# Routed experts at the end of a two-layer attention and FFN block: where expert numbers are loaded, what feeds the router, which engine splits the weights, and fill-in matmuls

## Chip, cores and metric

One core of one Trainium2 chip. The metric is the device time in microseconds (us) of one execution. The core has five instruction queues that run side by side and meet only at semaphores: TensorE (PE, with its weight loads PEld), VectorE (DVE), ScalarE (ACT), GpSimd (POOL) and SyncE (SP, which only starts transfers). A queue is worked off in order: what waits holds up all that stands behind it.

## What is computed

The stream x has 1024 tokens of 256 values. Two layers each add a gated cross attention and a gated FFN of normalised x. The change touches the end: the second layer's FFN, and the second attention only where weight work is laid beside it.

```python
x = x + tanh(g_xattn[1]) * L1_xattn(layernorm(x), ctx)
x = x + tanh(g_ffn[1]) * L1_ffn(layernorm(x))
# L1_ffn: 16 routed experts, top 2, and one shared expert
logits = xt @ Wr.T + bias;  probs = softmax(logits)
topk_val, topk_idx = top_k(probs, 2);  w = topk_val / (sum(topk_val) + EPS)
y[t, e] = (silu(xt @ Wg[e]) * (xt @ Wu[e])) @ Wd[e]
routed = sum over the chosen two of w * y
shared = (silu(xt @ sWg) * (xt @ sWu)) @ sWd
```

## The kernel before, in words

**Two-part numbers.** Each matmul operand is kept as an upper part (a rounded copy, `hi`) and a lower part (the rest, `lo`), and a product is three matmuls: hi*hi, hi*lo, lo*hi. ACT makes upper parts by copying (L1065 is its copy helper), DVE or POOL makes lower parts by subtracting.

**Second attention (`attention1`).** A loop over eight head pairs. POOL's only work in it is `normalise`: two multiplications for a pair (L430). After it `context_and_output` forms 16 context blocks, then eight output tiles of 128 tokens, each added to the stream `X` by DVE (`add_output`).

**Expert weights.** 16 experts and one shared expert are loaded in five groups (`WGROUPS`), the first at the start of `attention1`. Before the change all of them are split after the context: ACT copies the shared expert and experts 0 to 12 in one run, POOL subtracts the shared one and the even experts (L495), DVE the odd ones, one between two output tiles (`output_and_weights`, L1887). Experts 13 to 15 follow later.

**Layer norm 3.** For tiles 0 to 3, then 4 to 7, DVE computes statistics and an inverse root in a chain of small dependent operations (L1411 to L1418). Tiles are normalised by DVE (two) and ACT (two), transposed by PE (L578), copied by ACT to `xs[0]`, and DVE subtracts for `xs[1]` (`lower_part`).

**Routing.** The router needs whole numbers: POOL adds `xs[0]` and `xs[1]` to `xnT1` (`whole_stream`, L438), 512 tokens at a time, and PE multiplies by `wr` (`router`, L924). Then there is one chain: DVE picks two experts (`choice`, L1735 to L1750, its end is the count CHOSEN), PE ranks tokens within experts (`ranks`), DVE counts blocks, PE adds starts (`positions`), DVE gets each token's slot, a block number and a one-hot (`pk`, `beq`, `onehot`, L1764 to L1777), POOL forms `btok` from `beq` (L524), PE turns these into a list of tokens for each slot (`slot_tokens`), DVE converts it (`idxf`, `idx`, `eid`, L1785 to L1791). The slots are grouped into 31 blocks of 128, each of one expert. Work of the shared expert (`shared_gate_up`, `shared_hidden`, `shared_down`) stands between these steps on all engines.

**Blocks.** POOL gathers the 128 rows of a block by an indirect transfer (L532) into one of six buffers. PE takes blocks in 16 pairs: pairs 0 to 14 of two, the last of one. In pair i it loads two expert numbers from `eid` to registers (`expert_of`, a value_load), then `block_gate_up` of block 0 (six matmuls, L987 to L989, which find their weights by the register), `hidden_transposes(i-1)` (L998), `block_gate_up` of block 1, `block_transposes(i+2)` (L968), `block_down(i-1)` (six matmuls, L1011 to L1013). `block_down(i-1)` waits for `hTb_lo`, which comes from the hidden transposes by an ACT copy and a DVE subtraction (L1439). The results go to DRAM pair by pair.

**End.** After the last pair POOL gathers two result rows for each token (16 indirect transfers, L540), DVE adds them, SP writes the output.

`bridge(count, bank)` is a helper that was there before: PE multiplies a 128x128 identity by itself `count` times into an unused bank (L565). One such multiplication appears as two records in the trace.

Of the kernel before, what the change touches and what calls it, by code (L numbers as in the profile page):

```python
# [7 lines left out]
P = 128  # L8
# [46 lines left out]
def build(nc, x, kvT, kvTrot, kv, cosT, sinT, cosR, sinR, cosQ, sinQ, attn0, attn1, ffn0, ffn1,  # L55
          router0, router1, bias1, gates, ident_d, iota_d, tables, out):
    with ExitStack() as ctx:
# [183 lines left out]
        class SparseSems:  # L241
            def __init__(s):
# [3 lines left out]
                s.whi, s.wlo_p, s.wlo_d = sem(p + "whi"), sem(p + "wlo_p"), sem(p + "wlo_d")  # L246
# [16 lines left out]

        def width(i):
            return min(2, NBLK - 2 * i)
# [11 lines left out]
        def _(sp):  # L277
# [87 lines left out]
            for i in range(NPAIR):  # L365
                nb = width(i)
                sp.wait_ge(sparse.by, i + 1)
                sp.dma_start(y_dram[2 * i * P:(2 * i + nb) * P].rearrange("(b p) d -> p b d", p=P),
                             yout[:, i % YB, 0:nb * DM].rearrange("p (b d) -> p b d", b=nb)).then_inc(
                    sparse.y_out[i % YB], 16)  # L370
# [9 lines left out]
        def _(pool):  # L380
# [43 lines left out]
            def normalise(s):  # L424

                with pool.Fori(0, HP - 1) as i:
                    for h in range(2):
# [4 lines left out]
                            ALU.mult).then_inc(s.p, 1)  # L432

# [56 lines left out]
            def sparse_ffn():  # L490
                s = sparse

                def lower_weights(dst, raw, upper, count):
                    pool.wait_ge(s.whi, count)
                    nc.gpsimd.tensor_tensor(dst, raw, upper.bitcast(F32), ALU.subtract).then_inc(s.wlo_p, 1)  # L495

# [24 lines left out]
                for k in range(2):  # L521
                    for part in range(2):
                        tok = table[:, TTOK + part * NT:TTOK + (part + 1) * NT].unsqueeze(2).to_broadcast([P, NT, NCOL])
                        nc.gpsimd.tensor_tensor(btok[:, k * NT:(k + 1) * NT, part, :], beq[:, k * NT:(k + 1) * NT, :], tok,  # L524
                                                ALU.mult).then_inc(s.btok, 1)
# [3 lines left out]
                for j in range(NBLK):  # L529
                    if j >= XG:  # L530
                        pool.wait_ge(s.bt, (j - XG) // 2 + 1)
# [22 lines left out]
        def _(pe):  # L554
# [345 lines left out]
            def sparse_ffn():  # L900
                s, l = sparse, ln[3]

                def shared_gate_up(h):
                    tk = slice(h * HALF, (h + 1) * HALF)
                    for m in range(2):
                        for c in range(NCH):
                            col = (2 * c + m) * INTER
                            last = product(psum[2 * h + m][:, :], cut(WS, slice(None), slice(col, col + INTER)),
# [11 lines left out]
                def router(g):  # L920
                    pe.wait_ge(l.whole, l.before_whole + g + 1)
                    for t in range(4 * g, 4 * g + 4):
                        for c in range(NCH):
# [26 lines left out]
                def slot_tokens():  # L950
                    pe.wait_ge(s.btok, 4)
# [8 lines left out]
                def block_transposes(i):  # L960
                    for b in range(width(i)):
                        j = 2 * i + b
                        pe.wait_ge(s.got[j % XG], 16 * (j // XG + 1))
                    if i >= 2:
                        pe.wait_ge(s.bx, i - 1)
                    for b in range(width(i)):
                        for c in range(NCH):
                            last = nc.tensor.transpose(psum[2 + i % 2][:, b * DM + c * P:b * DM + (c + 1) * P],  # L968
                                                       xg[:, (2 * i + b) % XG, c * P:(c + 1) * P], ident[:])
                    last.then_inc(s.bt, 1)  # L970

                def expert_of(j):
# [55 lines left out]
                shared_down(2)  # L1028
                shared_down(3)
                slot_tokens()  # L1030
                pe.wait_ge(s.wlo_p, 11)
                pe.wait_ge(s.wlo_d, 6)
                pe.wait_ge(s.routed_dve, EXPERTS_OF)
# [29 lines left out]
        def _(act):  # L1063
# [43 lines left out]
            def context(s):  # L1107
                for b in range(NB):
                    act.wait_ge(s.c, b + 1)
                    copy(PT[0][:, :, b * S:(b + 1) * S],  # L1110
                         psum[b % 8][:].rearrange("p (h s) -> p h s", h=HP)).then_inc(s.c_hi, 1)

# [74 lines left out]
            def attention1():  # L1187
# [19 lines left out]

                body(0, first=True)
                with act.Fori(1, HP - 1) as i:
# [5 lines left out]
                context(s)  # L1215
# [68 lines left out]
            def sparse_ffn():  # L1284
                s = sparse

                def expert_upper(e):
                    copy(WE[:, e, 0, :], WE_raw[:, e, 1, :]).then_inc(s.whi, 1)

                def shared_gates(h):  # L1290
                    act.wait_ge(s.gu, 2 * h + 1)
                    nc.scalar.activation(silu1[:, h, :], psum[2 * h][:], ACT.Tanh, scale=0.5).then_inc(s.tanh, 1)
# [35 lines left out]
                act.wait_ge(s.ws, 16)  # L1328
                copy(WS[0][:], WS_raw[:]).then_inc(s.whi, 1)
                for k in range(4):  # L1330
# [3 lines left out]
                normalise(3, 0)  # L1334
                transposed_tiles(3, 0, (0, 1))
# [661 lines left out]
```

## Time and profile before

| | |
|---|---|
| median of 3 runs | 552.73 us (551.34 to 553.9) |
| the profiled execution | 552.05 us |
| its span in the trace | 550.3 us |
| busy: PE, DVE, ACT, POOL | 465.8, 400.2, 194.3, 172.8 us |
| mean granted clock of TensorE | 0.937 |

All times of rows count from the start of the span. In a timeline a row is: start, duration, engine, line, operation, out<-in with shapes, how many records were merged (x4), and in square brackets how long the engine had been idle before it and what ended that. The granted clock is 1.00 at 2.4 GHz and 0.50 at 1.2 GHz. 1.75 us of the profiled execution lie outside its span.

### The profile page before, as it was taken

To read this page: it belongs to the slowest core of one execution; us is meant where nothing else is said; L and a number is where in the kernel's file an instruction comes from. 1 tells how busy PE (TensorE), PEld (TensorE's weight loads), DVE (VectorE), ACT (ScalarE), POOL (GpSimd) and SP (SyncE) were. 2 spreads that over 40 slices of the span, in tenths; PEclk is the share of its full clock that TensorE was granted. 3 is DMA by queue.
4 is the path that set the end of the run, shared out by engine and by line. 5 is a ranking of instruction groups with operands and counts; after the bars stand their busy time and mean duration, and the time that the engine had idled before them with its cause. 6 is when DMAs were issued, how large, how long until landed. Compare 5 with 4: busy or idle time off the path is not lost.

```text
span 550.3 us, 8996 instructions
## 1 busy us (share of the span) xinstructions
PE 465.8 (85%) x3126; PEld 384.8 (70%) x3126; DVE 400.2 (73%) x838; ACT 194.3 (35%) x370; POOL 172.8 (31%) x149
## 2 busy tenths in 40 slices
PE   4499999999999999989998999999986818777600
PEld 4368667766865899978897888877986617776500
DVE  6988889889988946798679476879896774444323
ACT  3134222132332702434322456546914104445300
POOL 3815101101122001636530112120744476442064
PEclk9899999999999999999999999998997767999955
DMA  8302201220321100001105242223105014443234
GB/s 270 105 1 76 77 16 61 76 76 0 133 74 62 71 1 1 1 29 59 29 1 193 75 147 85 89 88 114 58 2 183 1 47 107 134 128 94 77 104 134
DMA packets 20287, 42.42 MB, mean 77 GB/s; under 512 B 3393, under 2 KB 10817, under 8 KB 20257
## 3 DMA queue, kind: packets, MB, share of 16 engines
q1 hardware_dynamic: 18000, 35.85, 19.6%
q0 software_dynamic: 2256, 6.16, 4.7%
q8 instruction: 19, 0.31, 0.2%
q14 instruction: 12, 0.09, 0.0%
HBM read 35.85 MB, written 6.16 MB: 76 GB/s over the span
## 4 chain that ended last, share of the span: by engine, by line
PE 52%; DVE 19%; issue 17%; POOL 6%; DMA 3%; ACT 2%; POOLq 0%; SPq 0%; DVEq 0%; ACTq 0%
PE ps L557 9%; PE ps L558 9%; PE ps L559 9%; PE ps L709 8%; POOL fg L540 2%; POOL probs L430 2%; PE ps L605 2%; PE ps L657 2%; PE ps L987 2%; DVE xT_lo L1439 2%; PE ps L989 1%; PE ps L988 1%; PE ps L615 1%; DMA W<-attn 1%; DVE rstd L1417 1%
## 5 line engine op out<-in xcount | busy, mean ns | idle before, releaser
L430 POOL TENSOR_TENSOR probs<-probs,rowrec 128x512 f32<-128x512 f32 x28 | 28.7, 1045 | 169.1 <-DVE rowrec L1477 168.9
L1065 ACT ACTIVATE PT_hi<-ps 128x512 fp32r<-128x512 f32 (+1 forms) x64 | 35.3, 604 | 54.6 <-PE ps L615 52.4
L557 PE MATMUL ps<-xs_hi,A_hi 128*128 128x512 f32 x128 | 52.4, 409 | 1.5 <-DVE xs_lo L1430 1.5
L558 PE MATMUL ps<-xs_lo,A_hi 128*128 128x512 f32 x128 | 50.4, 393 | 0.0
L559 PE MATMUL ps<-xs_hi,A_lo 128*128 128x512 f32 x128 | 50.3, 393 | 0.0
L1439 DVE TENSOR_TENSOR PT_lo<-ps,PT_hi 128x512 fp32r<-128x512 f32 (+1 forms) x64 | 40.8, 684 | 5.3 <-ACT PT_hi L1065 5.1
L532 POOL DMA_INDIRECT xg<-xn_rows,idx x31 | 29.6, 953 | 26.3 <-PE ps L968 18.6
L557 PE MATMUL ps<-N_hi,PT_hi 128*128 128x256 f32 x128 | 36.3, 284 | 0.0
L558 PE MATMUL ps<-N_lo,PT_hi 128*128 128x256 f32 x128 | 36.2, 282 | 0.0
L559 PE MATMUL ps<-N_hi,PT_lo 128*128 128x256 f32 x128 | 35.9, 281 | 0.0
L1465 DVE TENSOR_REDUCE rowmax<-ps 128x8 f32<-128x512 f32 x32 | 21.8, 683 | 16.8 <-PE ps L605 16.8
L987 PE MATMUL ps<-experts_split,xT_hi 128*128 x62 | 21.2, 341 | 13.6 <-DVE xT_lo L1439 13.2
L1065 ACT ACTIVATE G<-ps 128x512 f32<-128x512 f32 x32 | 18.9, 594 | 38.6 <-PE ps L709 34.8
L605 PEld LDWEIGHTS ps<-kbd,G 128*64 128x64 f32 x512 | 28.2, 137 | 5.6 <-issue 4.7
L605 PE MATMUL ps<-kbd,G 128*64 128x128 f32 x512 | 31.4, 275 | 0.0
L557 PEld LDWEIGHTS ps<-xs_hi,A_hi 128*128 128x128 f32 x128 | 24.3, 190 | 7.7 <-DVE xs_lo L1430 1.9
L1439 DVE TENSOR_TENSOR hTb_lo<-ps,hTb_hi 128x256 fp32r<-128x256 f32 (+1 forms) x16 | 6.7, 416 | 30.2 <-ACT hTb_hi L1065 30.2
L1085 ACT ACTIVATE probs<-probs 128x512 f32<-128x512 f32 x32 | 20.1, 629 | 23.6 <-DVE probs L1467 23.5
L559 PEld LDWEIGHTS ps<-xs_hi,A_lo 128*128 128x128 f32 x128 | 24.3, 190 | 5.4
L457 POOL TENSOR_TENSOR PT_lo<-qc,PT_hi 128x512 fp32r<-128x512 f32 x15 | 19.4, 1292 | 26.5 <-ACT PT_hi L1065 26.5
L558 PEld LDWEIGHTS ps<-xs_lo,A_hi 128*128 128x128 f32 x128 | 24.4, 190 | 4.5
L1071 ACT ACTIVATE qb<-X,shift,rstd 128x256 f32<-128x256 f32 x16 | 8.7, 594 | 52.7 <-DVE shift L1418 52.7
(222 smaller groups left out, 1351.4 us busy)
## 6 DMA issues: line engine op xcount, KB each, us to landing
W<-attn SPq DMA_DIRECT2D x8, 704.0 KB, 4.2
W<-attn SPq DMA_DIRECT2D x8, 672.0 KB, 4.0
W<-attn SPq DMA_DIRECT2D x16, 320.0 KB, 4.4
y_rows<-yout SPq DMA_DIRECT2D x15, 256.0 KB, 2.3
WF<-ffn SPq DMA_DIRECT2D x8, 384.0 KB, 4.1
experts_raw<-ffn SPq DMA_DIRECT2D x2, 1536.0 KB, 6.9
experts_raw<-ffn SPq DMA_DIRECT2D x2, 1152.0 KB, 5.8
X<-x SPq DMA_DIRECT2D x4, 256.0 KB, 5.0
```

What stands on the lines that cost most here:

```text
L430: nc.gpsimd.tensor_tensor(part, part, rowrec[:, 4 * h:4 * h + 4, :].unsqueeze(3).to_broadcast([P, 4, 2, L]), ALU.mult).then_inc(s.p, 1)
L532: nc.gpsimd.indirect_dma_start(out=xg[:, j % XG, :], out_offset=None, in_=xn_dram, in_offset=bass.IndirectOffsetOnAxis(ap=idx[:, j:j + 1], ...
L557: nc.tensor.matmul(dst, lhs[0], rhs[0], start=start, stop=False)
L558: nc.tensor.matmul(dst, lhs[0], rhs[1], start=False, stop=False)
L559: return nc.tensor.matmul(dst, lhs[1], rhs[0], start=False, stop=stop)
L605: last = nc.tensor.matmul(psum[6 + h][b * S:(b + 1) * S, t * P:(t + 1) * P], G[:, tok:tok + S], kbd[:, 2 * (4 * h + t) + b, :], start=True ...
L709: last = nc.tensor.matmul(psum[4 + h][a * DC:(a + 1) * DC, :], Wp[:, k, a * DC:(a + 1) * DC], rows[:, a, h * HALF:(h + 1) * HALF], start=( ...
L987: nc.tensor.matmul(out_, hi, w_hi, start=(c == 0), stop=False)
L1065: return nc.scalar.activation(dst, src, ACT.Copy)
L1085: nc.scalar.activation(part, part, ACT.Exp).then_inc(s.exp, 1)
L1439: V.tensor_tensor(dst, src, upper.bitcast(F32), ALU.subtract).then_inc(done, 1)
L1465: V.tensor_reduce(mx, sc, AX, ALU.max).then_inc(s.max, 1)
```

## The change

1. **Expert numbers.** The numbers of pairs 0 and 1 are loaded before `shared_down(2)`; those of pair i+2 inside pair i, one after each `block_gate_up`.
2. **Odd block first.** Pair 0 is now the one with a single block; pair i holds blocks 2i-1 and 2i.
3. **Router.** ACT copies the transposes from PSUM to `xnT1` (`whole`, 256 tokens at a time). POOL's two additions are gone; `router(1)` follows `router(0)` at once. The lower parts `xs[1]` of tiles 4 to 7 are made by POOL, not DVE.
4. **Weight splitting.** ACT splits the shared expert and experts 0 to 3 in the loop of `attention1`, 4 to 6 between context blocks, 7 to 15 after. POOL subtracts all 17.
5. **Order in the routing.** `shared_hidden(1)` moves on DVE from before the block counts to after `onehot`; the weights of the two choices (`mx[4]`, `cw`) move to after `eid`. ACT makes half of `btok`. POOL's `hidden_lower(1)` moves between the third and the fourth gather. On PE `positions` and `slot_tokens` move ahead of shared matmuls.
6. **Fill-ins.** `bridge` of 10, 8, 24 and 10 in `sparse_ffn`.

```diff
+        ODD = NBLK % 2
+        def first_of(i):
+            return max(0, 2 * i - ODD)
         def width(i):
-            return min(2, NBLK - 2 * i)
+            return 1 if ODD and i == 0 else 2
+        SHARED_BANK = (2, 0)
...
@@ POOL, normalise of attention1 @@
+                first = WGROUPS[0][1]
+                pair(0)
+                lower_weights(WS[1][:], WS_raw[:], WS[0][:], 1)
+                with pool.Fori(0, first) as e:
+                    pair(e + 1)
...
+                    lower_weights(lo, raw, hi, e + 2)
+                with pool.Fori(first + 1, HP - 1) as i:
+                    pair(i)
...
@@ POOL, sparse_ffn @@
-                lower_weights(WS[1][:], WS_raw[:], WS[0][:], 1)
-                for e in range(0, 13, 2):
+                for e in range(WGROUPS[0][1], WGROUPS[3][1]):
                     expert_lower(e)
-                pool.wait_ge(at[1].o, NT)
-                whole_stream(3, 0, xnT1)
-                whole_stream(3, 1, xnT1)
-                expert_lower(13)
-                expert_lower(14)
                 hidden_lower(0)
-                expert_lower(15)
-                hidden_lower(1)
+                for b in range(2):
+                    pool.wait_ge(ln[3].hi, ln[3].before + 2 + b + 1)
+                    tk = slice((4 + 2 * b) * P, (6 + 2 * b) * P)
+                    nc.gpsimd.tensor_tensor(xs[1][:, :, tk], xnT1[:, :, tk], xs[0][:, :, tk].bitcast(F32),
+                                            ALU.subtract).then_inc(ln[3].lo, 1)
+                for e in range(*WGROUPS[4]):
+                    expert_lower(e)
...
                 for j in range(NBLK):
+                    if j == 3:
+                        hidden_lower(1)
...
@@ PE, sparse_ffn @@
-                pe.wait_ge(s.wlo_p, 1)
+                pe.wait_ge(s.wlo, 1)
                 pe.wait_ge(l.lo, l.before + 2)
                 shared_gate_up(0)
+                bridge(10, 5)
                 transpose_tiles(3, 1, (6, 7))
                 router(0)
+                router(1).then_inc(s.routed_pe, 1)
+                bridge(8, 5)
                 pe.wait_ge(l.lo, l.before + 4)
-                router(1).then_inc(s.routed_pe, 1)
                 shared_gate_up(1)
                 ranks()
                 shared_down(0)
+                positions()
                 shared_down(1)
-                positions()
+                bridge(24, 2)
+                slot_tokens()
+                bridge(10, 2)
+                pe.wait_ge(s.routed_dve, EXPERTS_OF)
+                of = {i: [expert_of(i, b) for b in range(width(i))] for i in range(2)}
                 shared_down(2)
                 shared_down(3)
-                slot_tokens()
...
                 block_transposes(0)
                 block_transposes(1)
-                of = {}
                 for i in range(NPAIR):
-                    of[i] = [expert_of(2 * i + b) for b in range(width(i))]
...
-                    block_gate_up(i, 0, of[i][0])
-                    if i:
-                        hidden_transposes(i - 1)
-                    if width(i) > 1:
-                        block_gate_up(i, 1, of[i][1])
+                    for b in range(width(i)):
+                        block_gate_up(i, b, of[i][b])
+                        if i + 2 < NPAIR:
+                            of.setdefault(i + 2, []).append(expert_of(i + 2, b))
+                            if width(i) == 1:
+                                of[i + 2].append(expert_of(i + 2, 1))
+                        if i and b == 0:
+                            hidden_transposes(i - 1)
                     if i + 2 < NPAIR:
                         block_transposes(i + 2)
...
@@ ACT, attention1 @@
+                act.wait_ge(sparse.ws, 16)
+                copy(WS[0][:], WS_raw[:]).then_inc(sparse.whi, 1)
+                act.wait_ge(sparse.w[0], 16)
+                with act.Fori(0, first) as e:
+                    body(e + 1)
...
+                    copy(hi, raw).then_inc(sparse.whi, 1)
...
+                context(s, second_group)
...
@@ ACT, sparse_ffn @@
+                def whole(t, bank):
+                    src = psum[bank][:].rearrange("p (c k) -> p c k", c=NCH)
+                    copy(xnT1[:, :, t * P:(t + 2) * P], src).then_inc(s.whole, 1)
+                act.wait_ge(at[1].o, NT)
+                for b in range(2):
+                    act.wait_ge(ln[3].lo, ln[3].before + b + 1)
+                    whole(2 * b, b)
                 shared_gates(0)
                 normalise(3, 1)
+                for b in range(2):
+                    act.wait_ge(ln[3].tp, ln[3].before + 2 + b + 1)
+                    whole(4 + 2 * b, 6 + b)
                 transposed_tiles(3, 1, (6, 7))
                 act.wait_ge(s.w[4], 16)
                 expert_upper(13)
...
+                hidden_upper(0)
                 expert_upper(14)
-                hidden_upper(0)
                 expert_upper(15)
                 shared_gates(1)
...
+                act.wait_ge(s.routed_dve, BLOCK)
+                nc.scalar.activation(btok[:, :, 1, :], beq[:], ACT.Identity,
+                                     scale=table[:, TTOK + NT:TTOK + NT + 1]).then_inc(s.btok_act, 1)
...
@@ DVE, sparse_ffn @@
-                lower_part(3, 1, (6, 7))
+                shared_hidden(0)
                 dve.wait_ge(s.table, 16)
-                shared_hidden(0)
...
-                shared_hidden(1)
                 dve.wait_ge(s.routed_pe, RANKS)
...
+                shared_hidden(1)
                 dve.wait_ge(s.routed_pe, INDEX)
...
-            layer_norm(3, output_and_weights, (0, 1), lower_at=NT - 1)
+            layer_norm(3, lambda t: add_output(at[1], 1, t), (0, 1), lower_at=NT - 1)
```

## Rows read from the trace of the kernel before

**Rows 1.** The page: the chain that ended last, its shares by engine
```profile
PE 52%; DVE 19%; issue 17%; POOL 6%; DMA 3%; ACT 2%; POOLq 0%; SPq 0%; DVEq 0%; ACTq 0%
```
**Rows 2.** Stretches: bounds, us, busy PE, PEld, DVE, ACT, POOL, clock, DMA share, GB/s
```profile
446.00:455.00 9.00, 2.17 (x8) 1.43 (x8) 5.46 (x14) 1.06 (x2) 6.64 (x7) 0.50 0.33 84
455.00:517.00 62.00, 48.71 (x346) 44.29 (x346) 27.50 (x59) 27.23 (x58) 22.92 (x25) 0.96 0.41 110
```
**Rows 3.** Timeline of PE: pair 1, pair 6 and the start of 7, pairs 14 and 15
```profile
457.93 1.05 PE L968 MATMUL ps<-ident,xg 128*128 128x128 f32 x4
458.63 0.56 PE L987 MATMUL ps<-experts_split,xT_hi 128*128 x1
...
480.23 0.39 PE L987 MATMUL ps<-experts_split,xT_hi 128*128 x1 [0.95 <-DVE xT_lo L1439]
...
482.46 0.38 PE L1011 MATMUL ps<-experts_split,hTb_hi 128*128 x1
...
484.42 0.38 PE L987 MATMUL ps<-experts_split,xT_hi 128*128 x1 [0.98 <-DVE xT_lo L1439]
...
515.88 0.38 PE L1011 MATMUL ps<-experts_split,hTb_hi 128*128 x1 [0.31 <-DVE hTb_lo L1439]
...
517.19 0.38 PE L987 MATMUL ps<-experts_split,xT_hi 128*128 x1 [0.34 <-DVE hd L1812]
```
**Rows 4.** Timeline of PE: fill-ins before layer 2, transposes of layer norm 3, router
```profile
303.77 1.73 PE L565 MATMUL ps<-ident 128*128 128x128 f32 x14
...
408.10 1.24 PE L578 MATMUL ps<-ident,qb 128*128 128x128 f32 x8 [1.02 <-DVE qb L1422]
...
419.16 1.94 PE L578 MATMUL ps<-ident,qb 128*128 128x128 f32 x8 [2.18 <-DVE qb L1422]
...
425.04 3.57 PE L924 MATMUL ps<-wr,xnT 128*128 128x16 f32 x16 [0.72 <-POOL xnT L438]
```
**Rows 5.** Timeline of DVE: layer norm 3 and routing
```profile
415.00 1.40 DVE L1411 TENSOR_SCALAR varep<-meanvar 128x4 f32<-128x4 f32 x1
...
428.65 0.29 DVE L1745 TENSOR_TENSOR la<-ps,bias_s 128x128 f32<-128x128 f32 x1 [4.88 <-PE ps L924]
...
429.85 1.80 DVE L1737 SCALAR_TENSOR_TENSOR lb<-lb,table 128x128 f32<-128x128 f32 x1
...
434.27 0.29 DVE L1750 TENSOR_TENSOR mbf<-mk 128x128 bf16<-128x128 f32 x1
...
439.63 0.69 DVE L1772 TENSOR_TENSOR beq<-table,blk 128x512 f32<-128x512 f32 x1
...
445.80 0.23 DVE L1785 TENSOR_REDUCE idxf<-ps 128x32 f32<-128x64 f32 x1 [0.90 <-PE ps L955]
```
**Rows 6.** Timeline of POOL: one pair of attention1, then layer norm 3 and routing
```profile
348.59 2.04 POOL L430 TENSOR_TENSOR probs<-probs,rowrec 128x512 f32<-128x512 f32 x2 [6.50 <-DVE rowrec L1477]
...
413.98 2.40 POOL L438 TENSOR_TENSOR xnT<-xs_hi,xs_lo 128x1024 f32<-128x1024 f32 x1 [8.26 <-DVE xs_lo L1430]
...
428.39 1.27 POOL L503 TENSOR_TENSOR hT_lo<-hid,hT_hi 128x512 fp32r<-128x512 f32 x1
...
429.62 1.88 POOL L495 TENSOR_TENSOR experts_split<-experts_raw,experts_split 128x768 fp32r<-128x768 f32 x1
...
440.47 4.21 POOL L524 TENSOR_TENSOR btok<-beq,table 128x256 bf16<-128x256 f32 x4 [2.30 <-DVE beq L1772]
...
446.53 1.12 POOL L532 DMA_INDIRECT xg<-xn_rows,idx  x1 [1.86 <-DVE idx L1787]
```
**Rows 7.** Timeline of ACT: one pair of attention1; the weights after the context
```profile
346.36 0.38 ACT L1065 ACTIVATE Wp<-ps 96x256 f32<-96x256 f32 x1 [2.12 <-PE ps L586]
...
388.18 9.64 ACT L1065 ACTIVATE experts_split<-experts_raw 128x768 fp32r<-128x768 f32 x13
```
**Rows 8.** Chain in order of time: start, us, what: gather and last result
```profile
447.96 3.96 DMA xg<-xn_rows,idx
...
523.13 1.70 DMA y_rows<-yout
```

More of the change, by code:

```diff
@@ L424, in normalise, with pair @@
             def normalise(s):
-                with pool.Fori(0, HP - 1) as i:
+                def pair(i):
                     for h in range(2):
@@ L432, in normalise, with lower_weights @@
                             ALU.mult).then_inc(s.p, 1)
+                if s is at[0]:
+                    with pool.Fori(0, HP - 1) as i:
+                        pair(i)
+                    return
+                first = WGROUPS[0][1]
[3 more added lines that the diff above has]
+                    pair(e + 1)
+                    lo, raw, hi = (w[:, bass.ds(e, 1), part, :].rearrange("p a c -> p (a c)")
+                                   for w, part in ((WE, 1), (WE_raw, 1), (WE, 0)))
+                    lower_weights(lo, raw, hi, e + 2)
+                with pool.Fori(first + 1, HP - 1) as i:
+                    pair(i)
+            def lower_weights(dst, raw, upper, count):
+                pool.wait_ge(sparse.whi, count)
+                nc.gpsimd.tensor_tensor(dst, raw, upper.bitcast(F32), ALU.subtract).then_inc(sparse.wlo, 1)
             def whole_stream(n, h, dst):
@@ L521, in sparse_ffn @@
                 for k in range(2):
[L522 to L525, printed above, removed]
+                    tok = table[:, TTOK:TTOK + NT].unsqueeze(2).to_broadcast([P, NT, NCOL])
+                    nc.gpsimd.tensor_tensor(btok[:, k * NT:(k + 1) * NT, 0, :], beq[:, k * NT:(k + 1) * NT, :], tok,
+                                            ALU.mult).then_inc(s.btok, 1)
                 pool.wait_ge(s.routed_dve, TOKENS)
@@ L920, in router @@
                 def router(g):
-                    pe.wait_ge(l.whole, l.before_whole + g + 1)
                     for t in range(4 * g, 4 * g + 4):
+                        if t % 2 == 0:
+                            pe.wait_ge(s.whole, t // 2 + 1)
                         for c in range(NCH):
@@ L950, in slot_tokens @@
                 def slot_tokens():
-                    pe.wait_ge(s.btok, 4)
+                    pe.wait_ge(s.btok, 2)
+                    pe.wait_ge(s.btok_act, 1)
                     for q in range(2 * NT):
@@ L1105, in score_weights, with context @@
                      psum[bank][0:rows, 0:sets * P].rearrange("p (c d) -> p c d", c=sets)).then_inc(s.wp_ev, 1)
-            def context(s):
+            def context(s, meanwhile=None):
                 for b in range(NB):
@@ L1206, in body @@
                         t1_and_m(i + 1, 1)
+                first = WGROUPS[0][1]
                 body(0, first=True)
-                with act.Fori(1, HP - 1) as i:
+                act.wait_ge(sparse.ws, 16)
[3 more added lines that the diff above has]
+                    body(e + 1)
+                    hi, raw = (w[:, bass.ds(e, 1), part, :].rearrange("p a c -> p (a c)")
+                               for w, part in ((WE, 0), (WE_raw, 1)))
+                    copy(hi, raw).then_inc(sparse.whi, 1)
+                with act.Fori(first + 1, HP - 1) as i:
                     body(i)
@@ L1214, in attention1, with second_group, expert_upper @@
                 transposed(s, HP - 1, (6, 7))
-                context(s)
+                def second_group(b):
+                    k, after = divmod(b, 4)
+                    if after == 3 and k < 3:
+                        if k == 0:
+                            act.wait_ge(sparse.w[1], 16)
+                        expert_upper(WGROUPS[1][0] + k)
+                context(s, second_group)
+            def expert_upper(e):
+                copy(WE[:, e, 0, :], WE_raw[:, e, 1, :]).then_inc(sparse.whi, 1)
             def experts(n):
@@ L1285, in sparse_ffn @@
                 s = sparse
-                def expert_upper(e):
-                    copy(WE[:, e, 0, :], WE_raw[:, e, 1, :]).then_inc(s.whi, 1)
                 def shared_gates(h):
                     act.wait_ge(s.gu, 2 * h + 1)
-                    nc.scalar.activation(silu1[:, h, :], psum[2 * h][:], ACT.Tanh, scale=0.5).then_inc(s.tanh, 1)
+                    nc.scalar.activation(silu1[:, h, :], psum[SHARED_BANK[h]][:], ACT.Tanh, scale=0.5).then_inc(s.tanh, 1)
                 def hidden_upper(h):
@@ L1326, in block_rows @@
                     copy(yout[:, i % YB, 0:n], psum[6 + i % 2][:, 0:n]).then_inc(s.by, 1)
-                act.wait_ge(s.ws, 16)
-                copy(WS[0][:], WS_raw[:]).then_inc(s.whi, 1)
-                for k in range(4):
+                for k in (2, 3):
                     act.wait_ge(s.w[k], 16)
```

55 lines of the change are left out of this document (24 added, 31 removed).

## Prediction

> **What bounds the kernel now.** I read first the chain that ended last, by engine [rows 1]: TensorE holds half of it, but "issue", time in which an engine waits for nothing that the profile shows, holds 17%. So the next question is where TensorE stands still with its inputs ready. The stretches show two places [rows 2]: before the first pair (446 to 455) TensorE is busy for 2.17 of 9 us and the granted clock is 0.50; in the pairs (455 to 517) it is busy for 48.7 of 62 us at 0.96, and no other engine for more than 27.5. The timelines then show what it waits for. In the pairs, each starts about 4.18 us after the last (58.56 us for 14, from pair 1 to pair 15 [rows 3]). In the routing one chain runs through DVE, PE and POOL until the first gather at 446.53 [rows 6]. What comes before 400 is TensorE's or the attention loop's and has no part in the change but a little work laid into gaps; what comes after the last result (the final gathers) is not touched. So the sum has four terms: time of the first gather, from there to pair 1, the pairs, and the end.
>
> **Cover in the attention.** ACT gets 5 copies in the loop, POOL 5 subtractions. A copy is 9.64 / 13 = 0.74 us [rows 7] and stands where ACT is idle for 2.12 us in each pair [rows 7]. A subtraction is 1.88 us [rows 6] and POOL is idle for 6.50 us in each pair [rows 6]. I cost both at nothing; without that cover it would be 4 x 0.74 = 3 us for ACT. The three copies between context blocks delay the last of them by a few tenths, while TensorE still has output tiles to do: nothing.
>
> **Term 1, the first gather (446.53).**
> (a) Layer norm. The transposes of tiles 0 to 3 stood idle for 1.02 us at 408.10 [rows 4] for DVE, whose turn was lengthened by its expert subtractions; with these gone the wait goes. For tiles 4 to 7 the first small operation of the chain began at 415.00 and took 1.40 us [rows 5], ending with POOL's addition (413.98 + 2.40 = 416.38 [rows 6]). Now it can be held only by POOL's work on expert 12, whose upper part ACT makes after the transposes (now 407.0 to 408.0): I put POOL's end at 413.5. The transposes at 419.16 [rows 4] then start near 416.4, 2.8 earlier.
> (b) Logits. They were read at 428.65 [rows 5], after POOL's sum. Now: transposes 1.24 us as at 408.10 if the fill-ins keep the clock, 1.94 if not [rows 4], then 32 router records, at half clock 3.57 / 16 = 0.22 us each [rows 4], at full clock about 0.12, as the fill-in record has (1.73 / 14 [rows 4]). Logits at 421.5 to 424.8.
> (c) The choice, up to `mbf` (ended 434.56 [rows 5]). One of its operations took 1.80 us, from 429.85 to 431.65, because POOL's weight subtraction ran from 429.62 to 431.50 [rows 5, 6]; the like at 434.27 took 0.29. So an operation of DVE with two SBUF inputs waits for POOL's to end. Now POOL has six there: three of 512 columns (1.27 each) and three of 768 (1.88) [rows 6], 9.4 us from about 421.4 on, when ACT has made the upper part of `hid`. Eight of DVE's operations have two such inputs, and each lets one of POOL's pass first. CHOSEN comes near 432.7, 1.9 earlier than before; without that wait it would be 427. The Trainium skill (SBUF - State Buffer, section "SBUF: two separate sides") has the same as an exclusive lock, held for a whole instruction, and by it moving work to POOL is a cost in itself. By it the sum stays as it stands here.
> (d) From `mbf` to `beq` was 5.07 us [rows 5]; `shared_hidden(1)` (two operations like `beq`, 0.69 each) leaves. I take 3.6: `beq` at 436.3.
> (e) From `beq` to `idxf` was 6.17 us [rows 5], of which POOL's four `btok` took 4.21 [rows 6]. Two are left; the four one-hots, which take turns with them, end 3.5 us after `beq`; `shared_hidden(1)`, 1.4 us, now stands on DVE before `idxf`. That is 441.9, if TensorE is there. But 24 fill-ins stand in its queue before `slot_tokens`: 48 records are 5.9 us at 0.12 and 10.7 at 0.22. Begun near 435.5, they end at 441.3 to 446, and `idxf` comes 1.1 us later. I take a clock that rises on the way: 443.6. The gather follows `idxf` by 0.73: 444.3, **-2.2**. Bounds: -8 (no waits for POOL, full clock), 0 (half clock all along).
>
> **Term 2, gather to pair 1.** It was 458.63 - 446.53 = 12.1 us [rows 3, 6]. Pair 0 needs one block only, but `hidden_lower(1)` (1.27) stands before the fourth gather, and with it `shared_down(2)` and `(3)`, which TensorE must do before the first transposes. The fifth gather is issued after some 5.6 us of four issues of 1.12 and one 1.27, and lands 4.0 later [rows 6, 8], near 10; its transposes follow at half clock or full. 11.2 to 12.5; **-0.4**. The three loads of numbers there fall into TensorE's wait.
>
> **Term 3, the pairs.** From the first matmul of `block_down` to the first of the next pair: 482.46 to 484.42, 1.96 us, with two loads between; 515.88 to 517.19, 1.31, with one [rows 3]. So a load costs 0.65, and six matmuls with their addresses 0.66. In pair 1 at half clock the four transposes (457.93) run into the next matmul (458.63) although two loads lie between [rows 3]: a load hides where TensorE's sequencer is ahead of queued matmuls. At full clock six matmuls take what the sequencer needs to issue them, so it is hardly ever ahead. After the change each load follows six matmuls. What goes is the wait for `hTb_lo` that now stands beside the loads, not under them: the sequencer needs 3 x 0.66 + 2 x 0.65 = 3.28, and what six transposes and their waits need, which lies between 0 and 480.23 to 482.46 less two sixes, 0.91 [rows 3]. A pair takes 3.28 to 4.19; I take the middle, 3.73. Thirteen of them, one without loads or transposes (2.9) and 0.7 for a start at half clock are 52.1 instead of 58.56: **-6.5**.
>
> **Term 4, the end.** The last pair has two blocks now, not one. From 517.19 to the landing of its result (523.13 + 1.70 = 524.83 [rows 8]) were 7.64 us. Six more matmuls (0.7), twice the width for the small operations and a result twice as long add 1.2 to 1.8; **+1.2**, as the clock may hold.
>
> Sum: -2.2 - 0.4 - 6.5 + 1.2 = -7.9 on the profiled execution, 552.05 to 544.15, or 544.0. The median shown is 0.7 above that execution, so the forecast is about 1.6% below it.
>
> **Rivals.**
> *The loads hide altogether (0.20).* Then TensorE itself is the bound of a pair: 2.23 + 0.66 = 2.9 to 3.05. For: the two loads vanish in pair 1. Against: at full clock there is little queued. Time: 13 x 0.7 = 9 less, 535. The Trainium skill (TensorE: Matmul & The Clock Gate, section "Architectural detail: the array is 16x 32x32, not 1x 128x128") gives this engine a queue of 64 instructions, which speaks for it; no row here shows how far it fills.
> *The choice is not held by POOL (0.10).* If POOL's six operations run before the logits or DVE gets in between them, CHOSEN is at 427, 5.5 earlier: 538.5. For: the operation at 428.65, which reads PSUM, took its 0.29 beside POOL's 1.27 at 428.39 [rows 5, 6]. Against: the 1.80.
> *The loads do nothing by moving (0.13).* Each costs 0.65 wherever it is, and `hTb_lo` comes later by the first: 4.1 a pair, 549. For: sequencer time is only moved. Against: the wait that lies under them.
> *Half clock in the pairs (0.04).* With gaps of half a microsecond twice in a pair, the granted clock could fall to 0.50, as it did before pair 0 [rows 2], where TensorE mostly waited. Eighteen matmuls at about 0.21 and the transposes make 5.2 a pair: 13 x 1.5 = 19.5 more, 563, slower than before. It decides from 4.3 us a pair on. Against: 0.96 with a gap of about 1 us in each pair now.
> *The whole moves little (0.05).* Fill-ins at half clock and a fifth gather late eat term 1 and 2 while the pairs gain 2: 550.
>
> **How the numbers follow.** My forecast 0.48; the rivals 0.20, 0.10, 0.13, 0.04, 0.05. The time is that of the first. The range goes from the first rival's 535, a little lower since it can meet the second, to the third's 549: 534 to 549.5. A measurement of this kernel can tell about 0.5%, 2.8 us. Faster by more takes the first three and most of the third rival: 0.88; the same 0.07; slower 0.05.
>
> **What would show it.** The start of pairs 2 to 13 should be 3.6 to 3.9 us apart, two short gaps inside each rather than one long one; at 3.0 the loads are hidden, at 4.1 they only moved. The first operation of the choice should start near 422 and `mbf` end near 433, with single operations as long as POOL's. The first gather should come near 444, the transposes of tiles 4 to 7 near 416.4. The fill-ins of 24 should end after the last one-hot. Attention pairs should keep their length. I am wrong above all if the pairs do not shorten, or if the routing chain is shortened by far more than 2 us.

## The result and the profile after

The kernel after takes 537.04 us (median of 4 runs, 536.2 to 539.57) beside 552.04 us of the kernel before on the same chip: a ratio of 0.9733, 95% interval 0.9688 to 0.9779. The forecast was 544.0, range 534 to 549.5. The profiled execution has a span of 534.4 us against 550.3. The page's chain by engine shows where it went: "issue" fell from 17% to 10% [rows 1].

```profile
PE 65%; DVE 15%; issue 10%; POOL 7%; DMA 2%; ACT 1%; POOLq 0%; SPq 0%; DVEq 0%; ACTq 0%
```

The stretches that answer to [rows 2], ahead of the first pair and through the pairs (same columns): TensorE now works for 6.92 of 10.6 us ahead of them, at a granted clock of 0.76 instead of 0.50, and for 91% of the time in them, before 79%.

```profile
441.00:451.60 10.60, 6.92 (x52) 6.33 (x48) 6.73 (x20) 0.60 (x2) 7.74 (x8) 0.76 0.28 67
451.60:505.00 53.40, 48.46 (x360) 43.30 (x360) 30.15 (x63) 29.40 (x62) 23.03 (x25) 0.98 0.54 131
```

Timeline of PE, the places of [rows 4] and then those of [rows 3]: layer norm and router, the fill-ins in front of the token lookup, `shared_down(2)` and the start of pair 1, the transposes at which the ten pairs measured below begin, one steady pair from transposes to transposes, the transposes at which the ten end, the start of pair 15.

```profile
407.26 1.03 PE L604 MATMUL ps<-ident,qb 128*128 128x128 f32 x8
...
416.22 1.24 PE L604 MATMUL ps<-ident,qb 128*128 128x128 f32 x8
417.30 3.64 PE L951 MATMUL ps<-wr,xnT 128*128 128x16 f32 x32
...
434.70 6.23 PE L591 MATMUL ps<-ident 128*128 128x128 f32 x48
440.77 0.63 PE L983 MATMUL ps<-btok,onehot 128*128 128x64 bf16 x16
...
447.14 0.58 PE L583 MATMUL ps<-shared_hi,hT_hi 128*128 128x256 f32 x1 [3.42 <-POOL hT_lo L529]
...
453.50 0.63 PE L996 MATMUL ps<-ident,xg 128*128 128x128 f32 x4 [0.23 <-issue]
453.89 0.36 PE L1016 MATMUL ps<-experts_split,xT_hi 128*128 x1
...
462.16 0.63 PE L996 MATMUL ps<-ident,xg 128*128 128x128 f32 x4 [0.15 <-issue]
...
479.39 0.63 PE L996 MATMUL ps<-ident,xg 128*128 128x128 f32 x4 [0.19 <-issue]
479.77 0.36 PE L1040 MATMUL ps<-experts_split,hTb_hi 128*128 x1
...
481.17 0.28 PE L1018 MATMUL ps<-experts_split,xT_lo 128*128 x1
481.46 0.41 PE L1027 MATMUL ps<-ident,hd 128*128 128x128 f32 x2
...
482.31 0.28 PE L1018 MATMUL ps<-experts_split,xT_lo 128*128 x1
482.83 0.63 PE L996 MATMUL ps<-ident,xg 128*128 128x128 f32 x4 [0.23 <-issue]
...
496.43 0.63 PE L996 MATMUL ps<-ident,xg 128*128 128x128 f32 x4 [0.17 <-issue]
...
500.55 0.28 PE L1016 MATMUL ps<-experts_split,xT_hi 128*128 x1
```

The waits of about 1 us for `xT_lo` [rows 3] are gone. The idle time that the rows still show stands in front of the transposes of gathered rows, right behind the second load, is put down to "issue", and is at most 0.42 us. It is not all. A matmul of 0.28 us starts 0.12 after the one before it, so an idle time counted from the end of a row misses some 0.16 us. By the starts there are two short gaps in each pair, one behind each load: 481.17 to 481.46 and 482.31 to 482.83. Over the ten pairs they are 0.28 and 0.52 us on average, where 0.12 is the step without a load in between.

Over these ten pairs, from the transposes at 462.16 to those at 496.43, a pair takes 3.43 us; the same ten in the kernel before took 4.17:

```profile
469.50 0.60 PE L968 MATMUL ps<-ident,xg 128*128 128x128 f32 x4
...
511.15 0.38 PE L968 MATMUL ps<-ident,xg 128*128 128x128 f32 x2
```

Timelines of DVE and POOL, the places of [rows 5, 6]:

```profile
421.05 0.29 DVE L1813 TENSOR_TENSOR la<-ps,bias_s 128x128 f32<-128x128 f32 x1 [3.24 <-PE ps L951]
...
422.27 1.24 DVE L1806 SCALAR_TENSOR_TENSOR lb<-lb,table 128x128 f32<-128x128 f32 x1
...
424.81 1.81 DVE L1816 SCALAR_TENSOR_TENSOR pk<-mk,la 128x128 f32<-128x128 f32 x1
...
426.97 1.48 DVE L1805 TENSOR_TENSOR lb<-pk,mx 128x128 f32<-128x128 f32 x1
428.49 1.78 DVE L1806 SCALAR_TENSOR_TENSOR lb<-lb,table 128x128 f32<-128x128 f32 x1
...
430.95 0.29 DVE L1818 TENSOR_TENSOR mbf<-mk 128x128 bf16<-128x128 f32 x1
...
434.69 0.69 DVE L1834 TENSOR_TENSOR beq<-table,blk 128x512 f32<-128x512 f32 x1
...
441.44 0.22 DVE L1845 TENSOR_REDUCE idxf<-ps 128x32 f32<-128x64 f32 x1 [1.28 <-PE ps L983]
```

```profile
420.81 1.27 POOL L529 TENSOR_TENSOR hT_lo<-hid,hT_hi 128x512 fp32r<-128x512 f32 x1 [7.37 <-ACT hT_hi L1100]
422.04 2.58 POOL L539 TENSOR_TENSOR xs_lo<-xnT,xs_hi 128x512 fp32r<-128x512 f32 x2
424.59 5.53 POOL L462 TENSOR_TENSOR experts_split<-experts_raw,experts_split 128x768 fp32r<-128x768 f32 x3
435.53 2.16 POOL L548 TENSOR_TENSOR btok<-beq,table 128x256 bf16<-128x256 f32 x2 [5.41 <-DVE beq L1834]
442.16 1.12 POOL L558 DMA_INDIRECT xg<-xn_rows,idx  x1 [4.47 <-DVE idx L1847]
```

Each long operation of the choice ends 0.15 to 0.2 us after one of GpSimd's: 423.51 after 423.33, 426.62 after 426.43, 428.45 after 428.28, 430.27 after 430.12 (ends of the second, fourth, fifth and sixth subtraction, each group split evenly).

| term | forecast | measured | from |
|---|---|---|---|
| first gather | -2.2 | -4.37 | 446.53 to 442.16 |
| gather to pair 1 | -0.4 | -0.37 | 12.10 to 11.73 |
| pair 1 to pair 15 | -6.5 | -11.90 | 58.56 to 46.66 |
| pair 15 to the first final gather | +1.2 | +0.77 | 8.40 (525.59 - 517.19) to 9.17 (509.72 - 500.55) |
| the rest | 0 | 0.0 | 24.71 to 24.68 |
| sum | -7.9 | -15.9 | 550.3 to 534.4 |

### The profile page after: what moved, and what is told of

It reads as the page before. It is cut to its first block, busy times and chain, and to the rows that moved or that the text cites. A ratio compares the mean times of both kernels' runs of the same rounds, so it can differ in the third digit from the quotient of the medians.

```text
span 534.4 us, 9206 instructions
## 1 busy us (share of the span) xinstructions
PE 471.6 (88%) x3230; PEld 391.1 (73%) x3230; DVE 390.0 (73%) x830; ACT 196.2 (37%) x375; POOL 176.6 (33%) x153
## 4 chain that ended last, share of the span: by engine, by line
PE 65%; DVE 15%; issue 10%; POOL 7%; DMA 2%; ACT 1%; POOLq 0%; SPq 0%; DVEq 0%; ACTq 0%
PE ps L583 12%; PE ps L584 11%; PE ps L585 11%; PE ps L735 8%; PE ps L631 3%; POOL fg L566 2%; PE ps L683 2%; POOL probs L440 2%; PE ps L996 2%; PE ps L591 2%; PE ps L1016 1%; POOL experts_split L462 1%; PE ps L641 1%; PE ps L1017 1%; PE ps L604 1%
## 5 line engine op out<-in xcount | busy, mean ns | idle before, releaser
L462 POOL TENSOR_TENSOR experts_split<-experts_raw,experts_split 128x768 fp32r<-128x768 f32 (+1 forms) x16 | 29.3, 1844 | 29.0 <-ACT experts_split L1100 29.0
L584 PE MATMUL ps<-N_lo,PT_hi 128*128 128x256 f32 x128 | 36.1, 282 | 0.0
L591 PE MATMUL ps<-ident 128*128 128x128 f32 x196 | 25.6, 288 | 5.2 <-DMA ident<-ident_d 5.2
L591 PEld LDWEIGHTS ps<-ident 128*128 128x128 f32 x196 | 24.4, 203 | 5.8 <-DMA ident<-ident_d 5.2
```

Of the source, the lines that this page charges most:

```text
L584: nc.tensor.matmul(dst, lhs[0], rhs[1], start=False, stop=False)
L591: nc.tensor.matmul(psum[bank][:, 0:P], ident[:], ident[:], start=True, stop=True)
```

## The experiments

Profiled executions reach the third layer norm at times up to 7.5 us apart, and 7.3 apart in two kernels whose code is the same up to there (403.91 us with pieces and two bare loads, 411.25 with bare loads alone), so the routing is measured in each from the first transposes of that layer norm (less TensorE's idle time before them) to the first gather: 39.45 us in the kernel before (446.53 - 407.08), 34.90 in the one after (442.16 - 407.26). Seven more kernels below have the same routing and fill-ins: 35.28 us in four of them, 36.0 to 36.1 in three, so differences of 1 us say nothing here. A pair is the mean of the ten before the last transposes of gathered rows.

**Loads back at the start of their pair**, the rest of the change kept.

```diff
-of = {i: [expert_of(i, b) for b in range(width(i))] for i in range(2)}
+of = {}
...
 for i in range(NPAIR):
+    of[i] = [expert_of(i, b) for b in range(width(i))]
...
-            if i + 2 < NPAIR:
-                of.setdefault(i + 2, []).append(expert_of(i + 2, b))
```

> The kernel after, with only the loads of the expert numbers put back to the start of their own pair. Theory A (the place of the loads made the pairs shorter): from transposes to transposes a pair goes from 3.43 back to about 4.18 us, as in the kernel before; 11 to 13 pairs by 0.75 make the time 8 to 10 us longer, near 546. Theory B (the pairs gained from something else in the change, such as the earlier gathers, the odd block at the front or a clock that rises sooner): the pairs stay within 0.2 us of 3.43 and the time within 3 us of the kernel after, near 538.

546.89 us, ratio to before 0.9916 (0.9886 to 0.9945); pairs of 4.19 us. Theory A. The old wait is back, 1.0 us for `xT_lo` ahead of each pair. From transposes to transposes:

```profile
479.29 0.60 PE L996 MATMUL ps<-ident,xg 128*128 128x128 f32 x4
...
481.68 0.38 PE L1016 MATMUL ps<-experts_split,xT_hi 128*128 x1 [0.95 <-DVE xT_lo L1505]
...
483.44 0.60 PE L996 MATMUL ps<-ident,xg 128*128 128x128 f32 x4
```

**The loads alone**, in the kernel before.

```diff
-of = {}
+of = {i: [expert_of(2 * i + b) for b in range(width(i))] for i in range(2)}
 for i in range(NPAIR):
-    of[i] = [expert_of(2 * i + b) for b in range(width(i))]
...
     block_gate_up(i, 0, of[i][0])
+    if i + 2 < NPAIR:
+        of[i + 2] = [expert_of(2 * (i + 2))]
...
         block_gate_up(i, 1, of[i][1])
+    if i + 2 < NPAIR and width(i + 2) > 1:
+        of[i + 2].append(expert_of(2 * (i + 2) + 1))
```

> The kernel before, with the loads alone moved inside the pair two pairs ahead, nothing else of the change. Theory A (the place of the loads alone makes the gain of the pairs): pairs of about 3.4 us instead of 4.18, so 9 to 11 us less than the kernel before, near 542. Theory B (the loads gain only together with the rest): pairs above 3.9 us and less than 4 us of gain, 548 or more.

539.29 us, 0.9806 (0.9761 to 0.985); pairs of 3.37 us. Theory A. In medians beside their own kernel before (550.94), the loads alone give 11.65 us and the rest alone (the run above) 4.05; together 15.7, where the whole change gave 15.0. The two parts add, as far as medians of four runs that spread over 3 to 6 us can tell.

**Loads made twice.**

```diff
             of.setdefault(i + 2, []).append(expert_of(i + 2, b))
+            expert_of(i + 2, b)
```

> The kernel after, with every load inside the pairs made twice, the second into registers that nobody uses. Theory A (the sequencer sets the pair: its work of loads, addresses and waits is barely covered): each further load costs the 0.65 us read from the kernel before, 1.3 us a pair, pairs of about 4.7 us and 15 to 17 us more, near 553. Theory B (TensorE's own work sets the pair and the loads are hidden under queued matmuls with room to spare): pairs of at most 3.7 us and less than 4 us more.

560.18 us, 1.0143 (1.0089 to 1.0197); pairs of 4.86 us, slower than the kernel before. Theory A in the pairs. The time is 23 us above the kernel after, where A said 15 to 17; 18.2 of the profiled execution's 24 lie between the starts of pairs 1 and 15 (64.83 us against 46.66), 3.3 ahead of the third layer norm. TensorE stands still behind both places, and the rows put it down to "issue":

```profile
500.73 0.63 PE L996 MATMUL ps<-ident,xg 128*128 128x128 f32 x4 [1.03 <-issue]
...
503.38 0.41 PE L1027 MATMUL ps<-ident,hd 128*128 128x128 f32 x2 [0.60 <-issue]
...
505.57 0.63 PE L996 MATMUL ps<-ident,xg 128*128 128x128 f32 x4 [0.94 <-issue]
```

Two loads more cost 4.86 - 3.43 = 1.43 us, 0.72 a load; without loads the sequencer would need 3.43 - 2 x 0.72 = 1.99 us a pair.

**Loads left out.**

```diff
-            of.setdefault(i + 2, []).append(expert_of(i + 2, b))
+            of[i + 2] = fixed     # the numbers of pair 1
```

> The kernel after without the loads inside the pairs: from pair 2 on every pair uses the expert numbers of pair 1, so the weights of the wrong experts; addresses, matmuls and waits are as before. Theory A (the loads still cost a part of their 0.65 us each): pairs of 2.9 to 3.1 us, TensorE's own work, and 4 to 6 us less than the kernel after, near 532. Theory B (they are hidden altogether, and the 3.43 us come from addresses and waits): pairs stay near 3.4 us and the time within 1.5 us.

532.01 us, 0.9633 (0.9575 to 0.9691); eight steady pairs of 2.85 us, without a wait for "issue". Theory A: 2.85 us is TensorE's own time, and what stood above it is gone. The run leaves out more than it was meant to, though. With the numbers fixed the addresses were worked out once: the trace has 18 register operations for addresses of the blocks' matmuls (L1016, L1017, L1040, L1041), the kernel after 186. So 3.43 - 2.85 = 0.58 us is an upper bound for what two loads cost a pair. (The last transposes come 4.39 us after those before; the last two gathers take 7.0 and 8.1 us to land there.)

```profile
479.46 0.60 PE L996 MATMUL ps<-ident,xg 128*128 128x128 f32 x4
482.31 0.60 PE L996 MATMUL ps<-ident,xg 128*128 128x128 f32 x4
```

**Loads without the check of bounds; one load for two numbers.** The first form reused eight registers. Addresses worked out for a register's first number were kept, it seems, and later loads fell away: the traces have 8 loads instead of 31 in the version with two loads a pair, 5 instead of 16 in the other, and blocks from pair 4 on used the weights of earlier ones.

> The kernel after, with one load a pair that fills two registers with the numbers of both blocks, without the bounds check that follows each load. The runs before this one give 1.99 us of sequencer work a pair without loads and 0.72 us a load (4.87 us a pair with four loads, 3.43 with two), and 2.85 us for TensorE's own work. Theory A (the pair is the longer of sequencer and matmuls): 1.99 + 0.72 is under 2.85, so the pairs fall to 2.85 to 2.95 us and the time by 5 to 7 us, to 530 to 532. Theory B (two registers cost what two loads do): pairs of 3.2 us or more and less than 3 us of gain.

> The kernel after, with the same two loads a pair at the same places, but without the check of bounds (three register operations and an assertion) behind each. Theory A (the 0.72 us is mostly the load itself, the reading of memory): pairs of 3.2 us or more, at most 3 us of gain, 534 to 537. Theory B (it is mostly the instructions of the check): pairs of 2.85 to 3.0 us and 5 to 7 us of gain, 530 to 532.

530.77 and 530.04 us, 0.9624 (0.959 to 0.9659) and 0.9595 (0.9554 to 0.9635), steady pairs of 2.85 us in both. They come close to the run without loads and say nothing of a load's price. The same two with a register of its own for each number:

```diff
-    return pe.value_load(eid[0:1, j:j + 1], min_val=0, max_val=E1 - 1)
...
+    return [pe.value_load(eid[0:1, j:j + 1]).with_bounds(min_val=0, max_val=E1 - 1)]
```

```diff
+    into = [pe.alloc_register(f"number{i}_{b}") for b in blocks]
...
+    pe.reg_load(into if len(into) > 1 else into[0], eid[0:1, j:j + len(into)])
+    return [pe.snap(r, donate=True, min_val=0, max_val=E1 - 1) for r in into]
...
+            if i + 2 < NPAIR and b == 0:
+                of[i + 2] = experts_of(i + 2, range(2))
```

> The kernel after with all its 31 loads, each into a register of its own, at the same places, without the check of bounds behind each (three register operations and an assertion that needs two instructions). Theory A (the 0.72 us of a load is mostly the reading of memory): pairs of 3.2 us or more, at most 3 us less than the kernel after. Theory B (it is mostly the instructions of the check): 1.99 us of other sequencer work and two cheap loads stay under TensorE's own 2.85 us, pairs of 2.85 to 3.0 us and 5 to 7 us less, near 531.

> The kernel after with one load a pair that fills two registers, each of its own for every pair, without the check of bounds: 16 loads instead of 31. Theory A (a pair is the longer of sequencer and matmuls, and a load costs by the instruction): 1.99 us and one load stay under 2.85 us even at 0.72 us a load, so pairs of 2.85 to 2.95 us and 5 to 7 us less than the kernel after, near 531. Theory B (a load of two costs as two loads): no shorter than the kernel that keeps its 31 loads without the check, 3.2 us or more if that has them.

Without the check: 533.01 us, 0.9647 (0.9596 to 0.9698), pairs of 3.01 us, between the two theories. By the pairs a bare load, one without the check, costs at most (3.01 - 1.99) / 2 = 0.51 us, so the check is at least 0.21 of the 0.72. One load of two: 533.81 us, 0.9665 (0.9624 to 0.9707), pairs of 3.19 us. Theory A is out: one load a pair does not bring the pairs to 2.85.

The trace also has the register instructions of TensorE's own queue (PEldq). Load, check and assertion in the kernel after, then the load of two numbers (durations in ns: shortest, median, longest):

```profile
L1002 PEldq TENSOR_LOAD <-eid x31: 297/302/552, 443.4 to 495.7; - x31
L1002 PEldq FUSED_REGOPS  x31: 146/151/165, 444.0 to 496.0; - x31
L1002 PEldq SEQ_ASSERT  x31: 18/18/28, 444.4 to 496.2; - x31
```

```profile
L1003 PEldq TENSOR_LOAD <-eid x16: 491/534/546, 446.5 to 493.8; - x16
```

Filling two registers takes 0.53 us, filling one 0.30. From the start of a load to the next instruction of this queue behind it pass 0.68 us on average with the check, 0.36 to 0.40 without, 0.60 with two numbers. With 1.99 for the rest the sums of the last two are 2.75 and 2.59 us, under TensorE's 2.85, and the pairs are longer all the same. In these two kernels the queue needs 0.28 and 0.64 us on average to get past the wait for `hTb_lo` in front of `block_down`, in the kernel after 0.11. So the bounds from the pairs hold such a wait besides the load.

**GpSimd's subtractions in pieces** of 256 columns. The three of the weights are shown, the other three are cut alike.

```diff
+def expert_pieces(e):
+    pool.wait_ge(s.whi, e + 2)
+    for k in range(0, PACKF, PIECE):
+        cols = slice(k, k + PIECE)
+        last = nc.gpsimd.tensor_tensor(WE[:, e, 1, cols], WE_raw[:, e, 1, cols],
+                                       WE[:, e, 0, cols].bitcast(F32), ALU.subtract)
+    last.then_inc(s.wlo, 1)
...
 for e in range(*WGROUPS[4]):
-    expert_lower(e)
+    expert_pieces(e)
```

> The kernel after, with GpSimd's six subtractions beside the choice cut into pieces of 256 columns (2 for the hidden part, 4 for the layer norm's, 9 for the experts), the same work in all. Theory A (an operation of VectorE with two SBUF inputs waits for GpSimd's running instruction to end): the choice's long operations of 1.2 to 1.8 us fall to 0.4 to 0.8, and mbf ends 6 us after the first one, not 10.2; TensorE is then held by its own gate_up, so the first gather comes 2 to 3 us sooner, counted from the second layer norm, and the time is near 535. Theory B (the two engines share a path by bytes, whatever the instruction's length): mbf, gather and time as in the kernel after within 1 us.

532.18 us, 0.9644 (0.9616 to 0.9673). Theory A, with more gained than it said: layer norm to gather takes 30.76 us, 4.1 to 5.3 less than in the eight kernels with whole subtractions and fill-ins. The operations that took 1.24 to 1.81 take 0.70, though GpSimd's own work grew from 9.38 to 10.92 us. DVE and POOL of this kernel:

```profile
421.70 0.70 DVE L1826 SCALAR_TENSOR_TENSOR lb<-lb,table 128x128 f32<-128x128 f32 x1
...
423.17 0.70 DVE L1836 SCALAR_TENSOR_TENSOR pk<-mk,la 128x128 f32<-128x128 f32 x1
...
424.63 0.71 DVE L1826 SCALAR_TENSOR_TENSOR lb<-lb,table 128x128 f32<-128x128 f32 x1
...
426.12 0.72 DVE L1838 TENSOR_TENSOR mbf<-mk 128x128 bf16<-128x128 f32 x1
```

```profile
424.41 6.53 POOL L532 TENSOR_TENSOR experts_split<-experts_raw,experts_split 128x256 fp32r<-128x256 f32 x9
...
437.32 1.12 POOL L578 DMA_INDIRECT xg<-xn_rows,idx  x1 [3.11 <-DVE idx L1867]
```

**No fill-ins** between layer norm and pairs.

```diff
-                bridge(10, 5)
...
-                bridge(8, 5)
...
-                bridge(24, 2)
...
-                bridge(10, 2)
```

> The kernel after without the four groups of fill-in matmuls between the layer norm and the first pair. Theory A (they keep the clock up and cost little): router and shared matmuls fall to the lower clock, the logits come 2 to 3 us later, pairs 0 to 2 start at the lower clock, 2 to 4 us more in all, near 540. Theory B (the 24 in front of the token lookup delay it by what they gain elsewhere): logits later, but the lookup 1 to 2 us sooner after the last one-hot; the time within 1.5 us of the kernel after.

536.95 us, 0.9737 (0.9703 to 0.9771): the time of the kernel after. Theory B. Stretches of the kernel after, then of this one (same columns):

```profile
417.00:425.00 8.00, 6.14 (x53) 5.91 (x52) 4.52 (x9) 5.17 (x10) 4.19 (x4) 1.00 0.40 141
...
437.00:443.00 6.00, 6.00 (x68) 5.99 (x67) 4.62 (x9) 0.63 (x1) 1.53 (x2) 1.00 0.00 0
```

```profile
417.00:425.00 8.00, 6.70 (x33) 6.44 (x33) 2.32 (x5) 4.63 (x10) 4.76 (x4) 0.54 0.32 114
...
437.00:443.00 6.00, 1.34 (x16) 0.92 (x16) 5.86 (x11) 0.88 (x2) 2.90 (x3) 0.50 0.00 0
```

The fill-ins hold the full clock (1.00 against 0.54 and 0.50, the lower of 2.4 and 1.2 GHz), and the logits come 13.79 us after the layer norm's transposes instead of 16.12. That lead of 2.3 us runs into GpSimd's six subtractions, and what is left of it is spent behind the 24 fill-ins: gather 34.90 against 35.20, which is within what kernels with fill-ins differ by.

**Both cures together**, pieces with either form of load.

> The kernel after with GpSimd's six subtractions in pieces of 256 columns and with one load of two numbers a pair without the check of bounds. Theory A (the two act in different stretches, the choice and the pairs, so they add): 4.9 us less from the pieces and 5 to 6 us from the loads, 526 to 528. Theory B (the gathers, which give GpSimd 2.5 us of work for each pair, or the wait for the last weights become the bound once both are shorter): 529 or more, with TensorE waiting for a gather.

> The kernel after with GpSimd's six subtractions in pieces of 256 columns and with two loads a pair at their places, each without the check of bounds. Theory A (choice and pairs add, and two bare loads are better than one of two numbers): pairs of 3.0 us instead of 3.18, 14 times 0.17 less than the version with one load, 526 to 527.5. Theory B (a pair that short is bound by what feeds it, gathers or the small operations): no shorter than the version with one load, 528.5 or more.

With one load for two: 528.78 us, 0.9562 (0.9518 to 0.9607), layer norm to gather 30.88, pairs of 3.18. With two bare loads: 527.58 us, 0.9571 (0.9535 to 0.9608), 30.88, pairs of 3.02. The cures add: 537.0 less 4.9 and 3.2 is 528.9. The first of these times lies between its two theories; that the routing and the pairs both keep their gain, and that steady pairs show no wait for a gather, speaks for A. The two kernels cannot be told apart in time, so the second theory A is shown in the pairs and not in the time. They beat the kernel after by 8.3 and 9.5 us.

## Why the prediction was right, and where it was short

The mechanisms forecast for the routing and the pairs held; two terms were sized too small, and one came out right by another path.

**Cover in the attention** held. GpSimd's row of [rows 6] at 348.59 stands at 348.90, the last of that stretch at 365.99 (before 365.68), so its pairs keep their length. ScalarE's copy took 0.83 us there, out of an idle time that fell from 2.12 to 1.39.

**Term 1** was -2.2 and measured -4.37, or 39.45 - 34.90 = 4.55 counted from the layer norm; 3.4 to 4.2 in the seven other kernels with this routing (35.28 to 36.09). What makes these differ by 1 us stays open. Step (a) was exact (416.22, said 416.4). In (b) the logits came at 421.05, before the range of 421.5 to 424.8, because the clock held at 1.00 throughout. In (c) the mechanism is the one forecast: `mbf` waited on GpSimd's six subtractions, which ended at 430.12, and came at 431.24 instead of 432.7; from its logits to there were 10.2 us, and 6.4 in pieces. The Trainium skill (SBUF - State Buffer, section "SBUF: two separate sides") calls this an exclusive lock, held for the whole instruction, not a shared bandwidth. The runs agree: the waits shrank with the length of the instruction, 1.8 to 0.7 us, while the work grew. The rival in which the choice is not held is out. Step (d) took 3.45 of 3.6. In (e) the 24 fill-ins began sooner (434.70) and ran mostly at full clock, 6.23 us of the 5.9 to 10.7, and still made `idxf` wait for 1.28.

**Term 2** was exact in size (-0.37), though not by its path, so the size is partly luck. `hidden_lower(1)` did hold `shared_down(2)`, for 3.42 us (447.14), and the three loads fell into that wait. But the fifth gather had landed at 451.61. What held pair 1 were the two loads of pair 2's numbers, which stand one after the other behind the only block of pair 0: they run in TensorE's queue from 452.11 to 453.34, and the transposes start at 453.50.

**Term 3** is the step that failed in size: -6.5 forecast, -11.9 measured. The price of a load (0.65) was read rightly: the runs give 0.72, TensorE's own queue 0.68. Wrong was the amount for "six transposes and their waits", taken at the middle of 0 and 0.91. The 0.66 for six matmuls, read from 515.88 to 517.19, held a wait already besides the four address operations, so waits were counted twice. In the queue's records of the ten pairs 12 address operations take 1.59 us a pair, four waits 0.47 and two loads 1.36, together 3.42. Beside three times 0.66 and the loads that leaves less than 0.1 of the 0.45. That is 3.43 instead of 3.73, 3.0 us over ten pairs. The two short gaps inside each pair came as forecast.

The other 2.5 us are the first three pairs: 9.44 us from start to start (453.89 to 463.33), where 3 x 3.73 and 0.7 for half clock had been forecast. The clock was full (1.00), and the queue had less to do. The stretches between transposes there last 2.61, 2.85 and 3.19 us; they hold 8, 10 and 12 address operations and two, two and three waits, later ones 12 and four. Their loads take 1.28 to 1.32 us of the queue's time a stretch, about what they take later (1.29 to 1.54), so the loads do not hide there either.

So the rival in which the loads hide altogether was right on TensorE's own time (2.9 forecast, 2.85 without loads) and wrong on the loads: with them a steady pair is 3.43. Its time of 535 came nearer than the forecast of 544 by luck, since what was gained beyond the forecast came from the routing (2.2) and from the pairs by the amounts above (5.4). The rival of loads that gain nothing by moving is out (3.43, not 4.1), and so is half clock in the pairs (0.98).

**Term 4** was +0.77 for +1.2; the clock granted behind the last start was 0.90, before 0.76.

## What to carry to other kernels

Where an engine waits "for nothing" between short instructions with addresses from registers, count its sequencer's work as a second resource: the step takes at least the longer of the two sums, and a load of a register is dear (0.68 to 0.72 us here with its check) wherever the matmuls ahead of it run out. Moving work to GpSimd costs nothing only where VectorE has no operation at that time that GpSimd's instructions hold, above all none with two SBUF inputs; if it must stand there, cut it into short instructions. Fill-ins that raise the clock were worth nothing here (536.95 us without them, 537.04 with): look first whether what they speed up is held by another engine right after.

## What the runs showed of the hardware that was not expected

- A load of a number into a register of TensorE holds its queue for 0.68 us with a check of bounds (0.72 by the pairs with loads made twice), for 0.36 to 0.40 without; one load that fills two registers for 0.60.
- In the same queue an address operation, or a wait that is already met, takes 0.12 to 0.13 us: 12 and four of them in a pair are 1.59 and 0.47 us. Transposes add no such operation.
- GpSimd's subtraction of 256 columns takes 0.73 us against 1.84 for 768: 1.0 us more for the nine pieces, and VectorE's chain beside them is 3.8 us shorter.
- VectorE's operations with one input can be held too: beside the pieces a cast of 128x16 took 0.78 us and ended 0.04 after GpSimd's last piece (430.98 after 430.94); in the kernel after, with GpSimd idle, it took 0.17.
